# A megakernel's step times by kind of batch, and a ring of seven gather buffers

## The reference

```python
x = layernorm(x + attn0(x))   # q, k = silu; rotated; energy = q k^T * exp(slope * tril); RMS norm; gate u; output product
x = layernorm(x + ffn0(x))    # 2 layers: windowed attention (8 heads, window 64, softmax), then layer norm, gelu-gated FFN
x = layernorm(x + attn1(x))   # deformable sampling, below
x = layernorm(x + moe(x))     # softmax over the 1024 tokens, top 2 of 8 experts (3 products each), sums over tokens

# attn1
wave = silu(x @ wave_w.T + wave_b)            # freq and phase of each token
pos = clip(base + s_idx * freq_avg + phase_avg, 0, 1023)         # 33 samples per token
lo = floor(pos); frac = pos - lo
g = x[lo] + frac * (x[lo + 1] - x[lo])        # gathered rows
out = silu(einsum('blshd,blhs->blhd', g, silu(kernel weights)) @ out_w.T)
```

## Time and profile before

| what | value |
|---|---|
| median of 3 runs | 1969.92 us (1968.27 to 1970.03) |
| span of the profiled execution | 2353.6 us, core 0, mean granted TensorE clock 0.854 |
| busy in it | PE 1720.4, DVE 1254.1, ACT 988.0, POOL 1103.7 us |
| instructions | 31786 |

### The profile page before, as it was taken

One profiled execution on the slowest core, in us unless ns is written; L12 is line 12 of the kernel. 1 busy time (PEld: TensorE's weight loads), 2 busy tenths in 40 slices (PEclk: granted clock), 3 DMA queues, 4 the chain that ended last, 5 costly groups with the idle time before them and its releaser, 6 DMA issues.

```text
span 2353.6 us, 31786 instructions
## 1 busy us (share of the span) xinstructions
PE 1720.4 (73%) x12145; PEld 1141.7 (49%) x12153; DVE 1254.1 (53%) x2158; ACT 988.0 (42%) x2363; POOL 1103.7 (47%) x1069
## 2 busy tenths in 40 slices
PE   5787876767777766666776766667787768879866
PEld 3354534445445534344555434454455346656645
DVE  6565645555556444555565545655565454343345
ACT  3365673234543551243353540335354533343333
POOL 0000016475556345664556255554665367766630
PEclk8799998778989877988898978789888879989876
DMA  3010023132223232232223232232233343223321
GB/s 133 10 24 14 19 48 96 58 102 83 79 75 103 63 74 79 79 96 73 88 79 90 56 95 70 83 90 72 86 89 85 69 148 99 88 81 90 88 47 36
DMA packets 93420, 178.72 MB, mean 76 GB/s; under 512 B 21452, under 2 KB 50264, under 8 KB 93016
## 3 DMA queue, kind: packets, MB, share of 16 engines
q0 software_dynamic: 50688, 138.48, 21.4%
q1 hardware_dynamic: 42584, 38.23, 5.8%
HBM read 151.46 MB, written 9.44 MB: 68 GB/s over the span
## 4 chain that ended last, share of the span: by engine, by line
PE 39%; DVE 19%; another core or an unknown queue 18%; ACT 12%; issue 9%; SPq 1%; POOL 1%; DMA 1%; DVEq 0%; POOLq 0%; ACTq 0%
PE c L1612 5%; DVE pool_c L1235 4%; PE pa L1508 3%; PE pb L1508 3%; PE ta L1542 2%; DVE ssq L1132 2%; PE ta L1516 2%; ACT pool_a L771 2%; ACT pool_a L836 2%; PE sc L1587 2%; DVE pool_a L1155 1%; DVE pool_a L1185 1%; PE tb L1389 1%; PE pb L1560 1%
## 5 line engine op out<-in xcount | busy, mean ns | idle before, releaser
L729 POOL DMA_INDIRECT pool_c<-rows_of_x,idx x1056 | 1100.9, 1043 | 1156.5 <-PE c L1612 380.0
L1612 PE MATMUL c<-ident,pool_c 128*128 128x128 f32 x2112 | 337.1, 303 | 61.6 <-DVE pool_c L1235 32.2
L1612 PEld LDWEIGHTS c<-ident,pool_c 128*128 128x128 f32 x2112 | 278.3, 158 | 143.0 <-issue 97.0
L1235 DVE TENSOR_TENSOR pool_c<-pool_c 128x768 f32<-128x768 f32 x352 | 331.3, 951 | 20.1 <-DMA pool_c<-rows_of_x,idx 19.7
L860 ACT ACTIVATE prob<-sc,nmax 128x128 f32<-128x128 f32 x512 | 179.3, 374 | 0.1
L1516 PE MATMUL ta<-ident,pool_a 128*128 128x128 f32 x512 | 90.9, 333 | 90.8 <-DVE pool_a L1155 80.4
L771 ACT COPY pool_a<-tb 128x512 f32<-128x512 f32 x188 | 112.5, 599 | 103.6 <-remote 58.3
L1155 DVE TENSOR_TENSOR pool_a<-ta,rinv 128x512 f32<-128x512 f32 x64 | 44.3, 692 | 199.9 <-remote 158.3
L1542 PE MATMUL ta<-vmix,pool_a 128*64 128x64 f32 x1024 | 80.9, 239 | 81.0 <-ACT pool_a L771 67.5
L1142 DVE TENSOR_REDUCE nmax<-sc 128x8 f32<-128x1024 f32 x64 | 77.5, 1211 | 103.9 <-remote 96.1
L1508 PE MATMUL pa<-wqkv,pool_a 128*128 128x512 f32 x192 | 118.8, 706 | 12.9 <-DVE pool_a L1185 7.4
(11 more groups left out here) (413 smaller groups left out, 3344.3 us busy)
## 6 DMA issues: line engine op xcount, KB each, us to landing
pool_c<-rows_of_x,idx POOLq DMA_INDIRECT x1056
vmix<-vring SPq DMA_DIRECT2D x128, 128.0 KB
rows_of_x<-x2tok SPq DMA_DIRECT2D x16, 256.0 KB
xtok<-in_x SPq DMA_DIRECT2D x4, 512.0 KB
x_of_all<-x2tok SPq DMA_DIRECT2D x8, 256.0 KB
out<-pool_c SPq DMA_DIRECT2D x8, 256.0 KB, 2.3
wqkv<-in_wqkv SPq DMA_DIRECT2D x1, 1536.0 KB
xtok<-x_of_all SPq DMA_DIRECT2D x3, 512.0 KB
```

The source lines that it names most:

```text
L729: pool.indirect_dma_start(gat[:, n % GB, s, :], None, tables[b % 2], bass.IndirectOffsetOnAxis(ap=idx[:, t, SC * c + s:SC * c + s + 1], ax ...
L1235: V.tensor_tensor(g4, g4, wv, ALU.mult).then_inc(SEM["c_prod"], 1)
L1612: ins = mm(out[:, c:c + P], x, ident[:], start=(i == 0 and k == 0), stop=(i == BCH - 1 and k == len(parts) - 1), is_transpose=True, skip_g ...
```

## The change

There are now three kinds of batch (`KIND`: batch 0; batches 1 and 2; batch 3) and each kind has its own rows in `OPENING_AT`, `DENSE_AT`, `HEAD_AT` and `CHUNK_AT`, some with other times for single steps; three phases in `AT` are new. The ring of gathered rows has seven buffers. The space comes from `pos` and `lo`, which both halves of a batch now share, and from `zc`, which now lies on `cT`; ScalarE's copy into `cT` waits until the half before it has been read (`c_x3`). The numbers for kinds 0 and 2 are cut here except where they differ in a step named below.

```diff
-GB = 6
+GB = 7
...
-OPENING_AT = (-10.02, -8.96, -8.18, -7.82, -7.49, -7.26, -7.09, -6.96, -6.78, -6.42, -6.24, -6.23, -5.49, -4.17, -3.83, -3.72, -3.41, -3.27, -3.2, -2.79, -2.78, -2.77, -2.76, -2.75, -2.49, -2.42, -2.27, -2.26, -2.25, -2.24, -2.23, -2.22, -2.19, -2.18, -2.13, -0.83)
-DENSE_AT = ((5.59, 5.61, 5.89, 6.03, 6.23, 6.61), (9.33, 9.57, 9.81, 9.82, 10.54, 10.77), (14.63, 14.84, 15.16, 15.84, 16.08, 16.75, 17.15, 17.74), (18.22, 18.4, 18.45, 19.2, 19.51, 19.63, 20.16, 20.81))
-HEAD_AT = ((17.93, 17.99, 18.0, 18.13, 18.14, 18.21, 19.38), (21.23, 21.24, 22.92, 23.7, 24.34, 25.36))
+KIND = (0, 1, 1, 2)
+OPENING_AT = (
...
+    (-8.98, -8.96, -8.18, -7.82, -7.49, -7.26, -7.09, -6.96, -6.78, -6.42, -6.24, -6.23, -5.49, -4.17, -3.83, -3.41, -3.33, -3.27, -3.2, -2.79, -2.78, -2.77, -2.76, -2.75, -2.66, -2.65, -2.64, -2.63, -2.49, -2.46, -2.23, -2.22, -2.19, -2.09, -1.29, 0.01),
...
+DENSE_AT = (
+    ((5.59, 5.83, 5.89, 6.2, 6.23, 6.61), (9.33, 9.67, 9.81, 9.82, 10.54, 10.77), (14.63, 14.84, 15.16, 15.81, 16.08, 16.75, 17.15, 17.74), (18.22, 18.4, 18.45, 19.2, 19.58, 19.7, 20.05, 20.82)),
+    ((5.59, 5.61, 5.94, 6.2, 6.23, 6.61), (9.33, 9.57, 9.81, 9.82, 10.54, 10.77), (14.63, 14.84, 15.16, 16.08, 16.26, 16.75, 17.15, 17.74), (18.24, 18.4, 19.02, 19.14, 19.18, 19.49, 19.65, 20.24)),
...
+HEAD_AT = (
...
+    ((17.93, 17.99, 18.0, 18.13, 18.14, 18.21, 19.31), (20.95, 21.17, 22.31, 25.46, 26.02, 26.34)),
...
-CHUNK_AT = (19.61, 21.76, 23.16, 28.75, 33.26, 37.56, 41.27, 45.64)
+CHUNK_AT = (
...
+    (19.61, 21.76, 23.03, 28.75, 33.26, 37.55, 41.26, 45.64),
...
-    "pe": {"dense": 0.01, "proj": -1.95, "P": 1.06, "O": 1.27, "turn": -0.55, "v": -0.28, "oT": 1.72, "opening": -0.14, "S": -0.12, "wo": 1.9},
+    "pe": {"dense": 0.01, "proj": -1.95, "P": 1.06, "O": 1.24, "turn": -0.55, "v": -0.28, "oT": 1.72, "opening": -0.14, "S": -0.14, "wo": 1.91},
...
-    "dve": {"proj": -1.98, "O": 1.19, "rn": -1.71, "rot": -1.37, "wo": 1.78, "opening": -0.1, "R": 0.91, "S": -0.08, "dense": -0.03},
+    "dve": {"proj": -1.98, "O": 1.19, "rn": -1.71, "rot": -1.37, "wo": 1.78, "opening": -0.1, "R": 0.91, "S": -0.02, "dense": -0.03},
...
-    out = [(time + at["opening"], step) for time, step in zip(OPENING_AT, opening_steps())]
+    out = [(time + at["opening"], step) for time, step in zip(OPENING_AT[KIND[b]], opening_steps())]
...
-            out += [(time + at["dense"], step) for time, step in zip(DENSE_AT[J * l + j], steps)]
+            out += [(time + at["dense"], step) for time, step in zip(DENSE_AT[KIND[b]][J * l + j], steps)]
...
-        pos = part("c", T, S)
-        lo = part("c", T, S)
-        tmp = pos
+        pos = part("c", TB, S)
+        lo = part("c", TB, S)
...
-        zc = part("c", TB, D)
         cT = part("c", BLK)
+        zc = cT.rearrange("p (t d) -> p t d", d=D)
...
                 elif what == "cT":
+                    wait(act, "c_x3", b, TB * a[0])
                     copy_out(("sum", a[0]), cT[:, :], b)
...
-                p4, l4, f4 = pos[:, ts], lo[:, ts], frac.rearrange("p (t s) c -> p t s c", t=T)[:, ts]
+                p4, l4, f4 = pos[:], lo[:], frac.rearrange("p (t s) c -> p t s c", t=T)[:, ts]
```

More of the change, by code:

```diff
@@ L83 @@
 SECOND_LAYER = 9.0
-OPENING_AT = (-10.02, -8.96, -8.18, -7.82, -7.49, -7.26, -7.09, -6.96, -6.78, -6.42, -6.24, -6.23, -5.49, -4.17, -3.83, -3.72, -3.41, -3.27, -3.2, -2.79, -2.78, -2.77, -2.76, -2.75, -2.49, -2.42, -2.27, -2.26, -2.25, -2.24, -2.23, -2.22, -2.19, -2.18, -2.13, -0.83)
-DENSE_AT = ((5.59, 5.61, 5.89, 6.03, 6.23, 6.61), (9.33, 9.57, 9.81, 9.82, 10.54, 10.77), (14.63, 14.84, 15.16, 15.84, 16.08, 16.75, 17.15, 17.74), (18.22, 18.4, 18.45, 19.2, 19.51, 19.63, 20.16, 20.81))
-HEAD_AT = ((17.93, 17.99, 18.0, 18.13, 18.14, 18.21, 19.38), (21.23, 21.24, 22.92, 23.7, 24.34, 25.36))
-CHUNK = (0, 8, 9, 30, 45, 60, 75, 88)
-CHUNK_AT = (19.61, 21.76, 23.16, 28.75, 33.26, 37.56, 41.27, 45.64)
+KIND = (0, 1, 1, 2)
+OPENING_AT = (
[3 rows of a table added]
+)
+DENSE_AT = (
[3 rows of a table added]
+)
+HEAD_AT = (
[3 rows of a table added]
+)
+CHUNK = (0, 8, 9, 30, 45, 60, 75, 88)
+CHUNK_AT = (
[3 rows of a table added]
+)
 SUM_LAG = 0.42
 AT = {
[1 row of a table removed]
[1 row of a table added]
     "act": {"dense": 0.12, "P": 1.17, "rn": -1.72, "X": 0.44, "turn": -0.48, "v": -0.17, "oT": 1.83, "opening": -0.06, "proj": -2.05},
[1 row of a table removed]
[1 row of a table added]
 }
@@ L112, in opening_steps, with first_times @@
     return steps + [("mean", 1), ("shift", 0, 0), ("var", 1), ("shift", 0, 1)]
-def first_times(e):
+def first_times(e, b):
     at = AT[e]
-    out = [(time + at["opening"], step) for time, step in zip(OPENING_AT, opening_steps())]
+    out = [(time + at["opening"], step) for time, step in zip(OPENING_AT[KIND[b]], opening_steps())]
     for l in range(LAYERS):
@@ L132, in first_times, with chunk_time, second_times @@
     return out
-def chunk_time(n):
+def chunk_time(b, n):
     k = max(i for i in range(len(CHUNK) - 1) if n >= CHUNK[i])
-    return CHUNK_AT[k] + (CHUNK_AT[k + 1] - CHUNK_AT[k]) * (n - CHUNK[k]) / (CHUNK[k + 1] - CHUNK[k])
-def second_times():
+    at = CHUNK_AT[KIND[b]]
+    return at[k] + (at[k + 1] - at[k]) * (n - CHUNK[k]) / (CHUNK[k + 1] - CHUNK[k])
+def second_times(b):
     lag = {"acc": SUM_LAG, "cT": SUM_LAG + 0.05, "co": SUM_LAG + 0.1}
@@ L145, in second_times @@
     for j in range(J):
-        out += list(zip(HEAD_AT[j], second_head(j)))
-    out.append((HEAD_AT[0][-1], ("w", 0)))
+        out += list(zip(HEAD_AT[KIND[b]][j], second_head(j)))
+    out.append((HEAD_AT[KIND[b]][0][-1], ("w", 0)))
     for what, *a in second_steps()[HEAD:]:
         if what not in ("x2t", "wk", "pos"):
-            out.append((chunk_time(when(what, *a)) + lag.get(what, 0), (what, *a)))
+            out.append((chunk_time(b, when(what, *a)) + lag.get(what, 0), (what, *a)))
     return out
@@ L157, in schedule @@
     for b in range(B):
-        out += [(FIRST_AT[b] + time, ("first", b, *step)) for time, step in first_times(e)]
-        out += [(SECOND_AT[b] + time, ("second", b, *step)) for time, step in second_times() if b < B - 1 or time < TAIL_AT]
+        out += [(FIRST_AT[b] + time, ("first", b, *step)) for time, step in first_times(e, b)]
+        out += [(SECOND_AT[b] + time, ("second", b, *step)) for time, step in second_times(b) if b < B - 1 or time < TAIL_AT]
     return [step for _, step in sorted(out, key=lambda x: x[0])] + tail_steps()
@@ L239, in tail_steps @@
     late = second_head(1)
-    done = {step for time, step in second_times() if time < TAIL_AT}
+    done = {step for time, step in second_times(B - 1) if time < TAIL_AT}
     second = [("second", B - 1, *x) for x in late + [x for x in second_steps() if x not in late] if x not in done]
```

## The result

The new kernel takes 1933.76 us (median of 4, 1930.52 to 1937.52), the kernel before on the same chip 1969.1 us: a ratio of 0.9825, 95% interval 0.9806 to 0.9845.

What follows compares the result with a forecast made beforehand. Until 1870 us the chain through TensorE, VectorE and ScalarE sets the pace, then gathers and products are nearly level. Terms 2.0 + 2.8 - 3.0 + 2.7 + 3.0 + 3.0 = 10.5 us off 1969.92 give 1959.4; range 1941 to 1978.

Steps and rivals of the forecast that it cites:

- term 5: Ring of seven buffers: nothing until 1870 us, then POOL runs one chunk further ahead in the tail; 3.0 us gain.
- the 384 us beyond the median: The profiled execution lay 384 us above the runs' median; most unnamed waits were taken to exist only under the profiler.
- rival C: The ring counts: in shorter plain batches gathers come late, so a seventh buffer gives 18 us more, 1941 us; chance 0.14.
- the 18% of unnamed waits: Share of the span's chain of waits put on "another core or an unknown queue", taken as about 415 us.
- Term 1: Boundaries 1 to 2 and 2 to 3, xT now before ff 0: 1.0 us gain each, 2.0 in all.
- The bound of -1.8: Low end per later batch boundary: a loss of 1.8 us, from boundary 0 to 1's 8.25 us against 10.0 now.
- Term 2: mean 7 and var 7 earlier in kq 1 to 7, so the square waits less: 1.4 us gain twice, 2.8.
- Term 3: Opening ends, batches 1 to 3: pos 1, var 1, wk 6, wk 7 behind proj 0 0; 3.0 us loss, 2.7 gain.
- Rival B: Slower: pos 1 in the first tile holds turn 0 0, openings longer by 8.0 us, 1980 us; chance 0.18.
- Term 4: Score reductions behind a product in 15 places of batches 1 to 3, covering unnamed waits: 3.0 us gain.

Runs made afterwards that it cites:

- e1: The kernel before, unchanged, profiled a second time: 1968.66 us.
- e3: The new kernel with a ring of six instead of seven buffers (GB = 6): 1956.17 us, ratio to before 0.9934.
- e9: The new kernel with two instead of three gathers in every odd chunk from 7 on, 164 gathers fewer: 1901.56 us, ratio to before 0.9656.
- e10: The kernel before with the same 164 gathers left out, two instead of three in odd chunks from 7 on: 1917.89 us, ratio to before 0.9745.
- e4: The kernel before with a ring of five instead of six buffers (GB = 5): 2001.34 us, ratio to before 1.0186.
- e6: The new kernel with DENSE_AT of before: 1941.64 us, ratio to before 0.9844.
- e7: The new kernel with OPENING_AT and HEAD_AT of before: 1948.86 us, ratio to before 0.9891.
- e8: The new kernel with CHUNK_AT and the three phases in AT of before: 1946.35 us, ratio to before 0.9862.
- e2: The kernel before with a ring of seven buffers and the space they need, old tables kept: 1958.59 us, ratio to before 0.9954.

## Why the prediction was wrong

**The step that failed** is term 5 with the sentence under it, "Until 1870 us no product waits for a gather, so a deeper ring buys nothing: 0", and the bound it rests on, "So until 1870 us the first part's chain through TensorE, VectorE and ScalarE sets the pace". Both were read from an execution that was 387 us longer than the plain one of e1. There the other engines were late, so POOL kept ahead of them, and the ring waits (380 us) looked like POOL's slack. In the plain run gathers come late in every batch (43 times before the last batch), and a deeper ring pays: 9 us alone, and 21 us by the ratios on top of the new tables (e3 beside the result), where the term had 3.0 and all of it in the tail. Batch 1's gathers take 382.8 us from first to last: 281 busy, 79 of issue, 22.7 of ring waits (28.5 by the profile, less the 0.30 of issue in each of its 19), and nothing else. With the 16.2 us until the next indices that is the batch's period, 399 us. In the new kernel, counted the same way, it is 284 + 79 + 8.8 = 372, and with 18.6 of gap 391. This shows where POOL's time goes, not that POOL alone sets the period; e9 and e10 show that it does so in part.

The prediction had both signs in hand: the 384 us beyond the median, and that "all of a batch's gathers fill most of its time", which it left to rival C; and it named "the unnamed waits, if they hide what really bounds the plain run" as what would make it wrong. It took the 18% of unnamed waits as something to subtract, but kept the order of who waits for whom. That order was the part which the stretching had changed. (18% of 2353.6 us is 424 and not "about 415"; nothing rests on it.)

**Where the time went.** The starts of the 1st, 8th, 9th and 16th score reductions of a batch (L1142, now L1160) and of the first and last E (L1065, L1083) cut each batch into stages. Sums over batches 1 to 3, from the timelines of e1 and of after:

| stage | before us | after us |
|---|---|---|
| last tile to E 0 (boundary, kq, KV) | 269.9 | 269.7 |
| E 0 to E 3 | 47.6 | 43.2 |
| E 3 to first tile | 138.1 | 132.4 |
| first layer, tiles 0 to 7 | 321.1 | 305.8 |
| between the layers | 76.2 | 79.4 |
| second layer, tiles 0 to 7 | 326.9 | 322.3 |

That is 27.0 us; batch 0 gives 3.8 more and the tail 2.6. The first layer's tiles give most, 15.3. Their products wait 13.0 + 13.1 + 10.8 us for gathers in e1, and 7.5 + 5.8 + 9.6 in after: 14 us less. VectorE's next largest waits there are 3.1 and 4.4 us in a batch of e1, and 3.1 in one of after, so the late gathers are the likely price; with fewer gathers that stage falls to 291 us with the new tables and 294 with the old. In the tail it is not so: the products of the last batch wait 96.3 us for gathers in e1 and 63.7 in after, 33 us less, and the tail is 2.6 us shorter.

A part of the gain goes with TensorE's clock, which the terms don't have. TensorE's busy time falls from 1587.9 us in e1 to 1569.3 in after, with the same instructions (8 of its 12153 matmul records are missing in after), at granted clocks of 0.910 and 0.915. In the openings (first E to first tile, batches 1 to 3) the clock is 0.83, 0.82 and 0.84 in e1 and 0.86, 0.87 and 0.87 in after, in stretches that get 10.1 us shorter with 7 or 8 matmul records fewer in each. In the first layer's tiles of batches 1 and 2 the clock is 0.97 to 0.98 in both and can't be the cause. Among the 23 runs of before beside e1 to e4 (mean 0.909) a clock lower by 0.001 goes with 1.5 us; the four of after have 0.916, so an estimate of what goes with the clock is 10 of the 35 us. Whether the clock rises because waits are gone, or is worth something by itself, no run here separates.

**Term 1** (2.0 gain): the order of waits came as foretold, the sign of what it is worth did not. TensorE's timeline, boundary of batches 1 and 2, of e1 and then of after:

```profile
1130.71 2.08 PE L1560 MATMUL pa<-pool_a,w 128*128 128x512 f32 x2 [2.98 <-ACT pool_a L828]
...
1135.89 1.11 PE L1389 MATMUL pa<-ident,xtok 128*128 128x128 f32 x4 [1.39 <-DMA xtok<-in_x]
...
1145.52 2.81 PE L1569 MATMUL pb<-up,w 128*128 128x512 f32 x6 [1.85 <-DVE up L1166]
```

```profile
1116.43 1.12 PE L1407 MATMUL pa<-ident,xtok 128*128 128x128 f32 x4 [7.80 <-DMA xtok<-in_x]
...
1118.37 2.05 PE L1578 MATMUL pa<-pool_a,w 128*128 128x512 f32 x2
...
1127.08 2.81 PE L1587 MATMUL pb<-up,w 128*128 128x512 f32 x6
```

ff 0 waits behind xT, and ff 0 to down is 8.71 us (8.6 forecast). But the old leg, without unnamed waits, is 14.8 us and not 18.6. From the end of var (1130.66 and 1111.56 in ScalarE's timelines) to down it is 14.9 before and 15.5 after: a loss of 0.7 a boundary where 1.0 of gain was taken. The bound of -1.8, from the leg without unnamed waits, pointed this way. Four table loads fewer in all, as foretold; the groups of loads of e1 and of after:

```profile
L880 ACT ACT_TABLE_LOAD x27 | 34.6, 1283 | 0.5
L788 ACT ACT_TABLE_LOAD x10 | 12.8, 1283 | 0.1
```

```profile
L897 ACT ACT_TABLE_LOAD x25 | 32.1, 1283 | 0.4
L805 ACT ACT_TABLE_LOAD x8 | 10.3, 1283 | 0.1
```

A load is again 1.283 us. The Trainium skill, "ScalarE: Activation LUTs", section "What ACT_TABLE_LOAD costs", has the same 1.283 us for the load itself and adds a drain of about 1.38 us, 2.66 in all for a switch. The load agrees; the drain shows in no gap around it in e1's ScalarE rows:

```profile
1139.85 0.69 ACT L880 ACTIVATE lnq<-pa,cols 128x512 f32<-128x512 f32 x1 [1.37 <-PE pa L1560]
1140.55 1.28 ACT L788 ACT_TABLE_LOAD   x1
1141.85 0.69 ACT L788 ACTIVATE pool_a<-pa,kqb 128x512 f32<-128x512 f32 x1
```

From the end of the one function to the start of the other it is 1.31 us.

**Term 2** (1.4 a boundary) held. In ScalarE's timeline of after

```profile
1133.43 0.64 ACT L835 ACTIVATE lnq<-lnc 128x512 f32<-128x512 f32 x1 [1.95 <-DVE lnc L1124]
```

the square of mean 7 comes 6.35 us after down, and 7.91 in e1 (1153.43 after 1145.52): 1.6 us. That its wait would vanish was wrong: 2.33 us became 1.95. Terms 1 and 2 together are 0.9 a boundary, which fits an e6 that can't be told from nothing.

**Term 3** (3.0 loss, 2.7 gain) had its local prices right. The end of batch 2's opening in after, timelines of VectorE and TensorE:

```profile
808.06 0.57 DVE L1007 COPY pool_a<-x 64x512 f32<-64x512 f32 x1
822.05 0.22 DVE L1330 TENSOR_REDUCE pool_c<-pool_c 128x8 f32<-128x64 f32 x1 [0.16 <-ACT pool_c L914]
...
808.69 1.13 PE L1526 MATMUL pb<-wqkv,pool_a 128*128 128x512 f32 x2
...
827.52 1.86 PE L1534 MATMUL ta<-ident,pool_a 128*128 128x128 f32 x8
```

proj 0 0 follows the shift at once, and turn 0 0 comes 18.9 us after it, inside the 17 to 19 forecast (e1: 843.68 - 826.10 = 17.6). Rival B, which needed more than 22, is out. The sign was wrong all the same, since the term looked at the path from shift to turn and not at POOL: with both tables back (e7) the kernel is 10 us slower by its median (11 by the ratio, with some 10 of uncertainty), not 0.3 faster.

**Term 4** (3.0 gain): the cover it was built on isn't there in a plain run. The 96.1 us of unnamed waits before the score reduction are, in e1 and after, in VectorE's waits:

```profile
DVE nmax L1142 <- PE sc L1587: 8.5, 13, 2.2
```

```profile
DVE nmax L1160 <- PE sc L1605: 14.0, 6, 3.4
```

Putting these phases and `CHUNK_AT` back (e8) cost 7 us by the medians, within the intervals; what of it is the order of S is not known.

**Term 5**: the tail is 2.6 us shorter (3.0 taken). The 0 before it was the fault. The ring alone is worth 9 us; the step from five to six buffers is worth 31 by the medians (2001.34 against 1970.38) and 37 by the ratio.

**The rivals.** C, the ring counts, named the right condition ("if without the profiler's unnamed waits the batches are short enough that gathers come late") and had 18 us for it. The ring alone gave 9; what C did not have is that a new order of sums empties the ring sooner, and that both depend on each other.

**Left open:** which single step of `OPENING_AT` and `HEAD_AT` matters; each of the two tables alone is below what these runs can tell. And how much of the gain is the clock, and how much the waits. And the 17.3 to 18.6 us between batches in which POOL has no indices, some 54 us in all: they grew from 16.3 with the change. They grow with the seventh buffer and not with the tables: 20.0 us each in e2, 16.1 to 16.9 in e3. No kernel here made them clearly shorter. A kernel faster than after was not found among these, but for e9, which leaves gathers out.

## What to carry to other kernels

Compare a profile's span with the median before reading anything else. If it is much longer, its idle times and its order of who waits for whom are those of another run; busy times of POOL, VectorE and ScalarE hold (a gather 1.043 and 1.051 us, a product 0.95); those of TensorE did not, at granted clocks of 0.854 and 0.910 (a matmul of L1612 took 303 and 285 ns, one of L1508 on `pa` 706 and 654). Work out from those which engine is nearly full: here 264 gathers x 1.35 us = 357 of a batch's 390 us. Then read a ring's depth together with the longest stretch without a release (17 us here): the two changes gave more together than the sum of each alone. And take away some of that engine's work in an otherwise equal kernel before calling it the bound: 222 us less for POOL gave 32 and 51.

## What was not expected of the hardware

The same kernel had a profiled execution of 2353.6 us and one of 1966.5 us, at mean granted TensorE clocks of 0.854 and 0.910, with 31786 and 31794 instructions. Only in the longer one waits were put down to unnamed releases. TensorE's busy time was 1720.4 against 1587.9 us, so at most 133 of the 387 us are its own longer work. VectorE's was 1254.1 against 1253.7 and POOL's 1103.7 against 1112.8, so the rest sat in waits. What stretched it isn't known. The median of the plain runs (1969.92) had told that it was the odd one.
